# One count in the setup, copies on ScalarE, scalings on GpSimd, and a narrower wait in the last layer of a graph network

## The reference

```
h = maximum(layernorm(x), 0);  x = x + L0(h, edge_attr_3, edge_attr_64, ...)   # sums by src
h = maximum(layernorm(x), 0);  x = x + L1(h, node_vec1, edge_attr_4, edge_attr_8, ...)
h = maximum(layernorm(x), 0);  x = x + L2(h, node_vec1, edge_attr_16, edge_attr_4, ...)
h = maximum(layernorm(x), 0);  x = x + L3(h, edge_attr_16, edge_attr_4, ...)
```

```
msg   = (s_n @ Ws_src)[src] + (s_n @ Ws_dst)[dst]     (and the same for the vectors)
m1    = tensor_product(msg, edge_attr_4, edge_attr_16 @ W_rbf)
a     = sum(leaky(m1_s @ W_alpha) * alpha_dot);       alpha = softmax of a over the edges of a dst
val_s = m1_s @ Ws_val;  val_v = (m1_v @ Wv_val) * sigmoid(val_s @ Wg);  val_s = sigmoid(val_s)
m2    = tensor_product(val, edge_attr_4, w2);         h = m2 @ W_vlin
out   = node + (sum over the edges of alpha * h) @ Wp
```

## Time and profile before

| | |
|---|---|
| median of 3 timed runs | 7449.66 us |
| the three runs | 7449.66, 7432.34, 7451.65 us |
| the profiled execution | 7434.34 us |
| its span | 7432.50 us |
| its granted TensorE clock, mean | 0.94 |
| instructions | 115431 |

### The profile page before, as it was taken

The page is one execution under the profiler, slowest core; times in us unless marked ns, Lnnn a source line. Parts: engine busy times, 40 slices in busy tenths (PEclk is TensorE's granted clock), DMA queues, the critical chain, the costliest instruction groups (busy, mean ns, idle before and its releaser), DMA issues. The chain is left out here.

```text
span 7432.5 us, 115431 instructions
## 1 busy us (share of the span) xinstructions
PE 6825.7 (92%) x33582; PEld 4569.7 (61%) x33582; DVE 6524.0 (88%) x18559; ACT 3821.8 (51%) x10190; POOL 4867.5 (65%) x3538
## 2 busy tenths in 40 slices
PE   6999999999799999989999995699999999998488
PEld 3444444444555555555555553588888888887366
DVE  7999999999679988868888884699999999998884
ACT  2444444444333333343333332477777777776485
POOL 1777777777267777727777761788888888885000
PEclk6999999999689999989999997899999999999797
DMA  7999999999622222212222221444444444443363
GB/s 214 166 166 170 163 164 164 165 169 160 159 62 64 64 65 66 66 32 68 68 69 69 69 62 38 86 96 96 96 96 96 96 98 97 96 98 79 93 189 99
DMA packets 555487, 786.70 MB, mean 106 GB/s; under 512 B 94513, under 2 KB 406230, under 8 KB 554614
## 3 DMA queue, kind: packets, MB, share of 16 engines
q0 software_dynamic: 326592, 425.23, 35.4%
q1 hardware_dynamic: 224038, 353.46, 15.9%
q10 hardware_dynamic: 4240, 0.64, 0.1%
HBM read 472.16 MB, written 306.82 MB: 105 GB/s over the span
## 5 line engine op out<-in xcount | busy, mean ns | idle before, releaser
L674 POOL DMA_INDIRECT fore<-node_table,src_i x1664 | 1720.4, 1034 | 655.2 <-issue 505.3
L1574 DVE TENSOR_TENSOR work<-work 128x128 f32<-128x128 f32 (+6 forms) x4942 | 2016.3, 434 | 53.8 <-DMA work<-src_sum 27.1
L712 POOL DMA_INDIRECT src_sum<-work,put_i x832 | 1321.0, 1588 | 569.6 <-ACT work L906 396.4
L759 POOL DMA_INDIRECT fore<-src_table,put_i x784 | 1474.8, 1881 | 324.1 <-issue 190.8
L1328 PE MATMUL bank<-work 128*128 128x384 f32 (+1 forms) x3328 | 1208.7, 506 | 12.8 <-DVE work L1574 12.6
L1328 PEld LDWEIGHTS bank<-work 128*128 128x128 f32 x3328 | 607.6, 192 | 696.2 <-issue 312.8
L918 ACT ACTIVATE work<-bank 64x512 f32<-64x512 f32 x416 | 246.1, 592 | 1449.2 <-PE bank L1295 1449.2
L1574 DVE TENSOR_TENSOR work<-work,bank 128x384 f32 (+6 forms) x2080 | 899.2, 432 | 76.9 <-issue 67.3
L1280 PE MATMUL bank<-work 128*128 128x480 f32 x1664 | 791.2, 611 | 2.9 <-DVE work L1574 2.7
L1309 PEld LDWEIGHTS bank<-w_fc,work 64*128 64x128 f32 x3328 | 533.0, 188 | 237.9 <-issue 225.8
L1426 PE MATMUL bank<-ident,work 128*128 128x128 f32 x4704 | 650.3, 275 | 15.5 <-DVE work L1574 14.3
(11 more groups left out here) (277 smaller groups left out, 13115.7 us busy)
## 6 DMA issues: line engine op xcount, KB each, us to landing
edge_h<-work SPq DMA_DIRECT2D x196, 320.0 KB, 2.2
work<-edge_h SPq DMA_DIRECT2D x196, 320.0 KB, 3.4
work<-keys SPq DMA_DIRECT2D x196, 256.0 KB, 5.8
fore<-in_dst_row SPq DMA_DIRECT2D x196, 256.0 KB, 3.8
fore<-node_table,src_i POOLq DMA_INDIRECT x1664
work<-in_edge_attr SPq DMA_DIRECT2D x196, 128.0 KB, 5.8
src_sum<-work SPq DMA_DIRECT2D x4, 6240.0 KB, 37.6
work<-src_sum SPq DMA_DIRECT2D x100, 240.0 KB, 4.5
```

The lines of the kernel that those rows point to most:

```text
L674: return pool.indirect_dma_start(dst, None, table, bass.IndirectOffsetOnAxis(ap=idx, axis=0), bounds_check=bound, oob_is_err=True)
L712: pool.indirect_dma_start(src_sum[t], bass.IndirectOffsetOnAxis(ap=put_i[:, e:e + 1], axis=0), E.run[:, g % 2, t * 480:(t + 1) * 480], Non ...
L759: pool.indirect_dma_start(T.rows[:, b, t, :], None, src_table, bass.IndirectOffsetOnAxis(ap=put_i[:, e:e + 1], axis=0), compute_op=ALU.add ...
L1574: return V_.tensor_tensor(o, p, q, op)
```

## The change

Four edits, in the order of the program:

- **One count.** VectorE computes `next_lane` = partition number + 1, counts once, so that partition k holds the number of units whose window is below k+1, and puts the counts on the diagonal of `by_lane`. Before the products of block 9 (`COUNTED`) TensorE waits for this and spreads it with one matmul of 24 columns to all partitions; VectorE copies it into `before` ahead of block 9's rows. The 24 counts are gone, and the last blocks are taken over in one go.
- **Copies on ScalarE.** After the barrier ScalarE loads the 24 unit numbers into registers. At the end of its steps 8 to 31 of the first pass it makes the four copies for one border. VectorE waits for all 96 in `edges` of group 196, the first that uses them.
- **Scalings on GpSimd.** The 20 scalings go to GpSimd, in front of the barrier. It waits for `weights_ready`, and for its own earlier scalings where the same columns are scaled twice and before each of four on `rbf`.
- **The last layer's wait.** `m2` waits for `values_read` in place of `values_out`, and later, in front of L2314, for `sigmoid_out`. TensorE waits for `values_out` before each `turn_m2`.

```diff
@@ -44,6 +44,7 @@
 PAD_NODE = ROWS - 1
+COUNTED = 9
 S, V = 64, 32
@@ -225,7 +226,7 @@
-            "x_in", "blocks_zeroed", "weights_ready", "gate_weights_mm", 
+            "counts_ready", "borders_copied", "weights_scaled_early", "x_in", "blocks_zeroed", "weights_ready", "gate_weights_mm", 
             "keys_narrowed", "root_asked", "root_done", "table_in",
@@ -409,7 +410,7 @@
             v.columnI, v.trashI = g(P, dt=I32), g(2, dt=I32)
-            v.before, v.none, v.shift = g(MORE), g(MORE), g(MORE)
+            v.before, v.none, v.shift, v.by_lane, v.lower_units, v.next_lane = g(MORE), g(MORE), g(MORE), g(MORE), g(1), g(1)
             v.wide_dst = g(QK, P, dt=I32)
@@ -689,6 +690,35 @@
             pool.sem_inc(zero_made, 2)
+            def scale(w, by):
+                nc.gpsimd.tensor_scalar(w, w, by, None, ALU.mult).then_inc(s.weights_scaled_early, 1)
+                scale.n += 1
+            scale.n = 0
+            r3, r2 = 3 ** -0.5, 2 ** -0.5
+            pool.wait_ge(s.weights_ready, 1)
+            for l in (1, 2):
+                scale(wt[f"fc2_{l}"][:], 0.125)
+            scale(wt["fc2_0"][:, 160:192], r3)
+            scale(wt["fc2_0"][:, 192:224], r2)
+            for l in (1, 2):
+                scale(wt[f"in_s{l}"][:], 0.125)
+                scale(wt[f"in_v{l}"][:], 32 ** -0.5)
+                down = 96 ** -0.5 * (10 ** -0.5 if l == 1 else 1.0)
+                for w in ("out_s", "out_v"):
+                    scale(wt[f"{w}{l}"][:], down)
+                scale(wt[f"out_a{l}"][:], down * (0.1 if l == 1 else 1.0))
+            for row in (0, 32):
+                for by, c0 in ((r3, 160), (r2, 192)):
+                    pool.wait_ge(s.weights_scaled_early, scale.n)
+                    scale(wt["rbf"][row:row + 16, c0:c0 + V], by)
+            pool.wait_ge(s.weights_scaled_early, scale.n)
+            for l in (1, 2):
+                scale(wt[f"fc2_{l}"][:, 160:192], r3)
+            pool.wait_ge(s.weights_scaled_early, scale.n)
@@ -1027,7 +1057,22 @@
             barrier(act, "act")
-            unrolled(ALL_GROUPS, [(0, run_out), (-2, fc_out), (-3, relu_out)])
+            units = [act.alloc_register(f"act_unit{k}") for k in range(MORE)]
+            act.load(units, unit_i[0:1, 0:MORE])
+            def border_units(g):
+                k = g - 8
+                if not 0 <= k < MORE:
+                    return
+                unit, to = act.snap(units[k], min_val=0, max_val=UNITS - 1), TILES + 2 * k
+                for table in (src_i, src_f):
+                    act.activation(table[:, to:to + 2], table[:, 0:TILES].rearrange("p (u t) -> p u t", t=2)[:, bass.ds(unit, 1), :]
+                                   .rearrange("p o t -> p (o t)"), ACT.Copy).then_inc(s.borders_copied, 1)
+                for table in (y, aux):
+                    act.activation(table[:, to:to + 2, :].rearrange("p t c -> p (t c)"),
+                                   table[:, 0:TILES, :].rearrange("p (u t) c -> p u (t c)", t=2)[:, bass.ds(unit, 1), :]
+                                   .rearrange("p o c -> p (o c)"), ACT.Copy).then_inc(s.borders_copied, 1)
+            unrolled(ALL_GROUPS, [(0, run_out), (-2, fc_out), (-3, relu_out), (0, border_units)])
             for t in range(GROUP):
@@ -1186,6 +1231,10 @@
                     o = bank[:, place, :]
+                    if l == 0 and j == COUNTED:
+                        pe.wait_ge(s.counts_ready, 1)
+                        nc.tensor.matmul(o[:, 400:400 + MORE], U.one[:, 0:P], U.by_lane, start=True, stop=True)
                     if l == 0:
@@ -1477,6 +1526,8 @@
+                    pe.wait_ge(s.values_out, h + 1)
                     pe.wait_ge(s.m1_in_sbuf, min(h + 4, TILES // 2))
@@ -1702,6 +1753,8 @@
                     if l == 0:
+                        if j == COUNTED:
+                            V_.tensor_copy(U.before, o[:, 400:400 + MORE]).then_inc(dve_own, c.step())
                         V_.tensor_copy(row[:, 0:S], o[:, 0:64])
@@ -1741,7 +1794,12 @@
             V_.tensor_copy(U.window, window_i[:]).then_inc(dve_own, c.step())
+            V_.tensor_scalar(U.next_lane, U.lane, 1.0, None, ALU.add).then_inc(dve_own, c.step())
             dve.wait_ge(dve_own, c.n)
+            V_.scalar_tensor_tensor(U.is_lower, U.window, U.next_lane, U.one, ALU.is_lt, ALU.mult,
+                                    accum_out=U.lower_units).then_inc(dve_own, c.step())
+            dve.wait_ge(dve_own, c.n)
+            V_.tensor_scalar(U.by_lane, ident[:, 0:MORE], U.lower_units, None, ALU.mult).then_inc(s.counts_ready, 1)
             V_.tensor_reduce(U.n2, aux[:, 0:TILES, 0:3], AX, ALU.add).then_inc(dve_own, c.step())
@@ -1759,12 +1817,8 @@
                                     ALU.mult, ALU.add).then_inc(dve_own, c.step())
-            for k in range(MORE):
-                V_.scalar_tensor_tensor(U.is_lower, U.window, float(k + 1), U.one, ALU.is_lt, ALU.mult,
-                                        accum_out=U.before[:, k:k + 1]).then_inc(dve_own, c.step())
-                if k % 2:
-                    rows_to_sbuf(1)
-                dve.wait_ge(dve_own, c.n)
+            rows_to_sbuf(SLOTS)
+            dve.wait_ge(dve_own, c.n)
             V_.tensor_scalar(U.none, U.before, 0.5, 8192.0, ALU.is_lt, ALU.mult).then_inc(dve_own, c.step())
@@ -1785,16 +1839,6 @@
                 unit, to = taken(), TILES + 2 * k
-                V_.tensor_copy(src_i[:, to:to + 2], by_unit(src_i[:, 0:TILES])[:, bass.ds(unit, 1), :]
-                               .rearrange("p o t -> p (o t)")).then_inc(dve_own, c.step())
-                V_.tensor_copy(y[:, to:to + 2, :].rearrange("p t c -> p (t c)"),
-                               y[:, 0:TILES, :].rearrange("p (u t) c -> p u (t c)", t=2)[:, bass.ds(unit, 1), :]
-                               .rearrange("p o c -> p (o c)")).then_inc(dve_own, c.step())
-                V_.tensor_copy(src_f[:, to:to + 2], by_unit(src_f[:, 0:TILES])[:, bass.ds(unit, 1), :]
-                               .rearrange("p o t -> p (o t)")).then_inc(dve_own, c.step())
-                V_.tensor_copy(aux[:, to:to + 2, :].rearrange("p t c -> p (t c)"),
-                               aux[:, 0:TILES, :].rearrange("p (u t) c -> p u (t c)", t=2)[:, bass.ds(unit, 1), :]
-                               .rearrange("p o c -> p (o c)")).then_inc(dve_own, c.step())
                 V_.tensor_scalar(in_window[:, to:to + 2], by_unit(U.dst)[:, bass.ds(unit, 1), :].rearrange("p o t -> p (o t)"),
@@ -1806,22 +1850,6 @@
             r3, r2 = 3 ** -0.5, 2 ** -0.5
-            scale("fc2_0", r3, 160, 192)
-            scale("fc2_0", r2, 192, 224)
-            for l in (1, 2):
-                scale(f"fc2_{l}", 0.125)
-                scale(f"fc2_{l}", r3, 160, 192)
-                scale(f"in_s{l}", 0.125)
-                scale(f"in_v{l}", 32 ** -0.5)
-                down = 96 ** -0.5 * (10 ** -0.5 if l == 1 else 1.0)
-                for w in ("out_s", "out_v"):
-                    scale(f"{w}{l}", down)
-                scale(f"out_a{l}", down * (0.1 if l == 1 else 1.0))
-            for row in (0, 32):
-                for by, c0 in ((r3, 160), (r2, 192)):
-                    part = wt["rbf"][row:row + 16, c0:c0 + V]
-                    V_.tensor_scalar(part, part, by, None, ALU.mult).then_inc(dve_own, c.step())
-            dve.wait_ge(dve_own, c.n)
             for at, rows, col, by in ((64, 32, 0, r3), (96, 32, 1, r2), (32, 32, 2, r2), (96, 32, 2, r2)):
@@ -1861,6 +1889,9 @@
             def edges(g):
+                if g == GROUPS:
+                    dve.wait_ge(s.borders_copied, 4 * MORE)
                 b = g % 2
@@ -2303,7 +2334,7 @@
-                    dve.wait_ge(s.values_out, 2 * g + 2)
+                    dve.wait_ge(s.values_read, 2 * g + 2)
                     tt(vv, bc(cv[:, :, 68:100], 2, 3), bc(ys[:, :, 0:3], 3, V), ALU.mult).then_inc(dve_own, c.step())
@@ -2311,6 +2342,8 @@
                     dve.wait_ge(dve_own, c.n - 1)
+                    dve.wait_ge(s.sigmoid_out, 2 * g + 2)
                     tt(vv, vv, bc(f[:, :, 64:96], 2, 3), ALU.mult).then_inc(dve_own, c.step())
```

## The result

| | before | changed |
|---|---|---|
| median, six runs each | 7449.56 us | 7410.25 us |
| ratio of the two, 95% interval | | 0.9955 (0.9940 to 0.9969) |
| the same, timed again on another chip (e12, 17 and 12 runs) | 7748.48 us | 7724.65 us, 0.9971 (0.9960 to 0.9983) |
| profiled execution | 7434.34 us | 7420.74 us, span 7418.8 |

What follows compares the result with a forecast made beforehand. TensorE was taken to bound the last layer and VectorE alone the setup's end. Last layer -21.6, setup -11.9 and first pass +1.0 sum to -32.5 us, from 7442.0 to 7409.5 us (given as 7410); range 7387 to 7444.

Steps and rivals of the forecast that it cites:

- last layer, steady part: Last layer: the earlier signal removes TensorE's stalls, four groups take 43.06 us for 43.50, 49 x 0.44 = 21.6 us saved.
- copies to ScalarE, setup: Setup before the barrier: 96 copies leave VectorE's loop of 24 rounds, 10.0 us saved (0 to 12.8).
- scalings to GpSimd: Setup, between 119.14 and 123.44: the 20 scalings leave VectorE, 4.3 us saved.
- the count: Setup: one count replaces 24 without gain; work added ahead of TensorE's wait at 68.37 loses 0.95 us.
- GpSimd beside VectorE: Setup: GpSimd's scalings hold up VectorE's work beside them, 1.5 us lost (0 and 6 as ends).
- first pass: First pass: four small copies on ScalarE in each of 24 groups cost +1 us, mostly absorbed by its idle time.
- rival E: Last layer: TensorE's third wait costs time in each of 392 waits, +35 us, 7477; chance 5%.
- B: Last layer: the stall is not the signal's, four groups stay at 43.5; the setup alone gains, -11, 7431; chance 12%.
- that stays: Last layer: 0.30 us at TensorE's register load in one long group, taken to remain once the stall is gone.
- `in_window` steps: Setup: each of VectorE's 24 lone steps without the copies was priced at 0.24 us, between 0.13 and the whole round.
- Rival C: Setup's gain is given back, GpSimd holding VectorE or arriving last; only the last layer gains, -21, 7421; chance 8%.
- rival D: First pass: the copies delay each of 24 groups by 0.4 to 1 us, +10 to +24, 7419 to 7433; chance 9%.

Runs made afterwards that it cites:

- e12: The changed kernel once more on another chip, for more runs and a second trace: 0.9971 of the kernel before, four groups of the last layer 43.28 us.
- e5: The kernel before with the last layer's edit alone and TensorE's added wait doubled (values_out and values_read): 0.9983, four groups 43.29 us.
- e1: The kernel before with the last layer's edit alone: 0.9980 of the kernel before, four groups 43.28 us, last layer's stage 2240.8 us.
- e3: The kernel before with m2 waiting for values_read, then later values_out, and no added wait on TensorE: 0.9982, four groups median 43.29 us, stage 2248.8 us.
- e6: The changed kernel with TensorE loading eight registers every fourth half-group instead of sixteen every eighth: 0.9979 of the kernel before, four groups median 43.58 us.
- e13: The kernel before once more on another chip, for a second trace: setup 126.2 us, four groups 43.50 us, first pass 1761.9 us.

## Why the prediction was right, and where it was not

The time, the sign and the range held: 7410.25 for 7410. That it came so close is luck. The steps that the traces show add up to 20 to 26 us, not to 32.5, as the errors in the sum cancel only in part. The medians of the first timing happen to lie 39 us apart, more than either, and the level that I subtracted from, 7442, was 7.6 us under the median that the kernel before has. The right level and the measured steps give 7424 to 7430.

| step | forecast | measured |
|---|---|---|
| last layer, steady part | -21.6 | -10.8 (49 x 0.22) |
| last layer, its end | 0 | -4 |
| copies to ScalarE, setup | -10.0 | -12.0 |
| scalings to GpSimd | -4.3 | -4.6 |
| the count | +0.95 | +0.4 (+1.0 up to the last rows, -0.6 at the register load) |
| GpSimd beside VectorE | +1.5 | 0 |
| first pass | +1 | +5 to +11 |
| sum | -32.5 | -20 to -26 |

The sum of the measured steps is near the 22 of the second timing and reaches the interval of the first (23 to 45) only at that interval's low end.

- *The last layer* had the right mechanism: the signal came early enough, the waits for `m1` went from 64 to one, TensorE is next late, the third wait is free (rival E falls by e5, and B by the 43.28 of e1). The size failed at "that stays": I took the 0.30 us behind the register load as independent of the stall. The two overlapped, and 0.52 is what the load costs by itself. Half of the 0.44 was never to be had. The end of the stage gave 4 us that I had left out: between the last `edge_w3` but one and the barrier 40.6 us for 44.5, and 40.6 in e1 too. I take it that the last groups have nothing beside them, so that VectorE's wait counts in full; that is argued, not shown.
- *The setup* was mis-sized in the `in_window` steps, 0.155 each for my 0.24: I took too little from the row that was nearest, the pitch of 0.133, and leaned to the whole round. The count cost what I said, and the load of registers that "stays" took 0.6 us of it back. Rival C's contention did not show at the path at all. The rule beside it, that the two engines contend (the Trainium skill's "GPSIMD Engine Reference", section "8. Key points"), did show, but on the other engine: GpSimd ran three times as long as I gave it, some 6 us of that because VectorE held it, and the rest because a free scaling takes 0.22 to 0.71 us.
- *The first pass* was wrong in kind: I looked for a cost at the copies (rival D) and found none there, while all groups became a little longer. No rival had that. So some of the setup's gain seems to be given back later, by a third to two thirds; why is open.
- *The profiled pair* would have misled: -13.6 us. The stages that no edit touches moved by 7 or 8 us each way (117.5 or 125.4, 147.7 or 154.0).

## What to carry to other kernels

A stall ahead of a fixed cost on the same queue may be covering it: before adding up stalls, look whether a group without them has the fixed cost at its full size, and count only stalls in groups that have none. When a bound is lifted, read the engine that was far behind it too: here GpSimd's own instructions became 17% longer in another phase against VectorE and ate the gain. A median over a stage can hide such a change of pace in the middle of it, as in e3; compare the stage's length too. And where one stage varies by more than the change is worth, compare stages over many traces, not totals of two.

## What the runs showed of the hardware

- A GpSimd indirect DMA instruction of one line takes 1.73 us on average in one alignment against VectorE and 2.03 in another, single ones 3.05 for 1.54; e3 shows both in one execution, and e6 only the second.
- It holds from both sides. A VectorE comparison that takes 0.28 us free takes up to 0.65 beside a GpSimd scatter and then ends 0.47 us ahead of the scatter's end (50 of 50 in two traces); a GpSimd scaling that takes 0.28 us free took 2.65 beside a VectorE product and ended 0.14 us after it.
- Sixteen registers loaded on TensorE's queue show as 0.52 us of idle weight loading beyond the usual 0.28; eight, or four, show as none. Satisfied semaphore waits there, up to two more in each half-group, show as none either.
- Chips can differ in the clock that they grant in some stages alone. The second pass of the kernel before on the first chip and on the chip of e12 and e13:

```profile
2084.60:3216.80 1132.20, 1118.18 (x3744) 611.45 (x3744) 1009.55 (x2427) 389.48 (x1041) 867.66 (x832) 0.98 0.27 64
```

```profile
2075.40:3379.60 1304.20, 1208.39 (x3744) 650.54 (x3744) 1019.14 (x2427) 389.23 (x1041) 887.83 (x832) 0.90 0.22 56
```

50 us at half clock became 248, and 1132 us became 1304; in the third pass 29 us became 214 and 1121 us became 1282. The last layer's first pass, 2256.1 us on both, did not move. These two passes are the whole difference of 332 us between the two traces, and it has nothing to do with the change.
